# Score pass of the first batch in three attention stages: each score product made three times into the same bank

## The reference, cut to what matters

```python
q = split_heads(queries @ Wq + bq)          # 16 heads of 8
k = split_heads(keys @ Wk + bk)
scores = jnp.einsum('bhqd,bhkd->bhqk', q, k) / jnp.sqrt(jnp.float32(HD))
scores = jnp.where(mask, jnp.float32(-1000000000000000.0), scores)
attn = jax.nn.softmax(scores, axis=-1)
ctx = jnp.einsum('bhqk,bhkd->bhqd', attn, v)
```

## Time and profile before

| what | value |
|---|---|
| median of three runs | 1589.42 us (1583.72 to 1591.42) |
| the profiled execution, its time | 1584.89 us |
| its span, first to last instruction | 1581.8 us |
| mean granted PE clock over the span | 0.94 of 2.4 GHz |
| PE busy | 88% of the span |
| DVE, ACT, POOL busy | 65%, 54%, 34% |
| share of the chain that ended last: PE, DVE, POOL | 67%, 12%, 10% |

### The profile page before, as it was taken

The page is one execution under the profiler, slowest core; times in us unless marked ns, Lnnn a source line. Parts: engine busy times, 40 slices in busy tenths (PEclk is TensorE's granted clock), DMA queues, the critical chain, the costliest instruction groups (busy, mean ns, idle before and its releaser), DMA issues.

```text
span 1581.8 us, 21944 instructions
## 1 busy us (share of the span) xinstructions
PE 1386.6 (88%) x7201; PEld 1099.5 (70%) x7201; DVE 1028.4 (65%) x2075; ACT 850.9 (54%) x1608; POOL 545.0 (34%) x880
## 2 busy tenths in 40 slices
PE   3899798798999999889999997699989989875992
PEld 3565576554888888756678885588878878765992
DVE  4545678755666666845567775577777877655773
ACT  1244566355555555334577775456656666443661
POOL 6723511512233325332201103332333343332674
PEclk7699899799999999989999998889999999986996
DMA  6130232122622323311122100310000000133963
GB/s 153 33 92 2 61 114 94 41 80 63 193 101 99 113 88 120 103 38 61 45 50 107 54 1 1 118 42 1 1 12 5 1 16 1 36 139 117 382 249 87
DMA packets 67790, 123.13 MB, mean 78 GB/s; under 512 B 10200, under 2 KB 43792, under 8 KB 66399
## 3 DMA queue, kind: packets, MB, share of 16 engines
q1 hardware_dynamic: 40495, 104.57, 20.0%
q10 hardware_dynamic: 24688, 12.70, 3.0%
q0 software_dynamic: 2496, 4.47, 0.8%
HBM read 82.61 MB, written 29.16 MB: 71 GB/s over the span
## 4 chain that ended last, share of the span: by engine, by line
PE 67%; DVE 12%; POOL 10%; issue 7%; ACT 2%; DMA 2%; ACTq 0%; POOLq 0%; DVEq 0%; SPq 0%
PE psum L2003 11%; PE psum L2005 11%; PE psum L2004 11%; PE psum L2248 5%; PE psum L2388 4%; PE psum L2390 4%; PE psum L2389 4%; PE psum L2483 3%; PE psum L2201 2%; PE psum L2202 2%; POOL y_dram L994 2%; POOL slots_dram L963 2%; DMA shared<-in_mask_dram 1%; PE psum L2028 1%; PE psum L2232 1%
## 5 line engine op out<-in xcount | busy, mean ns | idle before, releaser
L1816 DVE TENSOR_TENSOR hhl<-psum,hhl 128x512 fp32r<-128x512 f32 x336 | 230.2, 686 | 83.6 <-ACT hhl L1282 81.5
L1282 ACT ACTIVATE hhl<-psum 128x512 fp32r<-128x512 f32 x336 | 199.3, 593 | 3.4 <-DVE psum L1812 3.2
L2003 PE MATMUL psum<-xh,wl 128*128 128x512 f32 x464 | 189.2, 408 | 3.2 <-DVE hhl L1816 2.5
L2004 PE MATMUL psum<-xl,wh 128*128 128x512 f32 x464 | 184.7, 398 | 0.0
L2005 PE MATMUL psum<-xh,wh 128*128 128x512 f32 x464 | 184.4, 397 | 0.0
L1062 POOL TENSOR_SCALAR shared<-shared,xstat 128x589 f32<-128x589 f32 x128 | 97.7, 765 | 232.4 <-DVE xstat L1906 231.9
L1272 ACT ACTIVATE psum<-psum 128x512 f32<-128x512 f32 x208 | 120.9, 582 | 71.3 <-PE psum L2005 70.0
L1354 ACT ACTIVATE hhl<-psum 128x512 fp32r<-128x512 f32 (+1 forms) x160 | 95.4, 596 | 116.9 <-PE psum L2483 116.6
L2388 PE MATMUL psum<-hhl,wl 128*128 128x512 f32 x336 | 135.0, 402 | 12.8 <-DVE xn L1836 9.4
L1812 DVE TENSOR_TENSOR psum<-act_out,psum 128x512 f32<-128x512 f32 x128 | 89.0, 696 | 84.0 <-PE psum L2005 78.5
L1911 DVE TENSOR_TENSOR hhl<-psum,hhl 128x512 fp32r<-128x512 f32 (+1 forms) x160 | 110.3, 689 | 49.6 <-ACT hhl L1354 49.0
(11 more groups left out here) (404 smaller groups left out, 3605.4 us busy)
## 6 DMA issues: line engine op xcount, KB each, us to landing
w3late<-w_dram SPq DMA_DIRECT2D x24, 768.0 KB, 7.2
abkb<-w_dram SPq DMA_DIRECT2D x18, 768.0 KB, 7.4
w_dram<-shared SPq DMA_DIRECT2D x16, 768.0 KB, 5.9
shared<-comb_dram SPq DMA_DIRECT2D x10, 1024.0 KB, 4.7
slots_dram<-late ACTq DMA_DIRECT2D x1, 9792.0 KB, 36.6
shared<-comb_dram SPq DMA_DIRECT2D x24, 256.0 KB, 5.0
late<-in_f_dram SPq DMA_DIRECT2D x8, 768.0 KB, 5.4
shared<-in_f_dram SPq DMA_DIRECT2D x8, 768.0 KB, 8.0
```

Source lines behind the costliest of these rows:

```text
L1282: a.activation(hh[k % 4], h_bank(f, k), ACT.Copy).then_inc(f.hh_done, 1)
L1816: v.tensor_tensor(hl[k % 4], h_bank(f, k), hh[k % 4].bitcast(f32), ALU.subtract).then_inc(f.h_ready, 1)
L2003: mm(dst, ll, rh, start=start, stop=False)
L2004: mm(dst, lh, rl, start=False, stop=False)
```

## The change

For batch 0 of each of the three stages, each score product is preceded by two more of the same operands into the same bank. Each of the three starts afresh (`start=True`), so the first two are overwritten, and the mask product is added to the third as before. Nothing is removed or moved, and no wait is added.

```diff
                         dst = bank(o + j, GW)
+                        if b == 0:
+                            for again in range(2):
+                                mm(dst, qst(l, b)[0:KS, 2 * half + j, tq], kst[0:KS, b, half, at:at + GW],
+                                   start=True, stop=True)
                         mm(dst, qst(l, b)[0:KS, 2 * half + j, tq], kst[0:KS, b, half, at:at + GW], start=True, stop=False)
                         ins = mm(dst, maskT[:, mask_slot(l, b), tq], spreadb[:, 0:GW], start=False, stop=True)
```

## The result

The changed kernel took 1591.44 us (median of 20 runs, 1586.00 to 1595.18) against 1585.78 for the kernel before (20 runs beside it, 1580.78 to 1592.95). The ratio is 1.0034 with a 95% interval of 1.0019 to 1.0049, so it is slower by 5.4 us, between 3.0 and 7.8. In the first three runs the kernel before had its median at 1589.42; the forecast was 1597 us, which was 7.5 us on top of that. The absolute number is therefore 5.6 us too high, of which 3.6 us is that first median; the shift is 2.1 us too large.

What follows compares the result with a forecast made beforehand. PE, busy 88% of the span and 67% of the chain, was taken to bound the kernel. Stages 3.0 + 2.6 + 2.6 = 8.2 us, less 0.7 for the clock, gave 7.5 on 1589.4: 1597 us, range 1588 to 1606.

Steps and rivals of the forecast that it cites:

- The price of a product and the count: Batch 0 steps: 96 added products, each 0.142 us at full clock and 0.26 at low; 13.7 to 25.0 us in all.
- rival of low price: All three stages: nothing is hidden and every step costs 1.04 us, up to 25 us, 1614 in total; chance 0.07.
- What hides: Stage 1 step 0 hides in PE's 3.10 us wait; stage 2 step 0 in 0.81, steps 1 and 2 in 0.92.
- Stage 0: Batch 0 steps of stage 0: nearly all added time on the path; 3.0 us, between 0.4 and 6.0 by the clock.
- Stages 1 and 2: Batch 0 steps there: 2.6 us each, from 2.3 to 3.5 in stage 1 and 2.3 to 3.7 in stage 2.
- Step 7 adds 0.57 ... 2.3 to 3.5: End of stage 1: step 7 adds 0.57 us and gets 0.8 back if the clock holds longer, or adds 1.04.
- The clock given back: Start of the second pass: how long the clock stays low there; 0.7 us taken off the sum.
- the clock holds: Hand-over to the second pass: busier PE keeps the clock from falling in any stage; -2.8 us, 1586.6; chance 0.17.
- a delay was absorbed later: Behind the stages: PE waits later for POOL or a transfer, where the shift ends; 0 to 3 us, 1591; chance 0.12.

Runs made afterwards that it cites:

- again: The changed kernel once more, unaltered, against the kernel before: ratio 1.0034 (1.0014 to 1.0054, 12 runs), +5.4 us.
- again2: The changed kernel a third time, unaltered, against the kernel before: ratio 1.0067 (1.0043 to 1.0091, 6 runs), +10.6 us.
- five: Each score product of batch 0 five times instead of three, 192 products added, against the kernel before: ratio 1.0134, +21 us.
- batch1: The 96 extra products in the steps of batch 1 instead of batch 0, against the kernel before: ratio 1.0065, +10.3 us.
- early: Extra products only in steps 0 to 2 of stages 1 and 2 (24 products), against the kernel before: ratio 1.0002 (0.9983 to 1.0020).
- s0: Extra products in stage 0 alone (32 of the 96), against the kernel before: ratio 1.0031, +4.9 us.
- s12: Extra products in stages 1 and 2 alone (64), against the kernel before: ratio 1.0017, +2.7 us.
- free: No extra products; POOL's first weight splits of stages 1 and 2 wait until DVE has split batch 0's maxima; against the kernel before: ratio 0.9967.
- free_triple: The extra products of the change, with POOL's splits of stages 1 and 2 waiting for batch 0's maxima, against the kernel before: ratio 1.0028, median 1591.09 us.
- fill: No tripling; POOL's splits wait, and unread score products fill PE's waits at batch 0's hand-over; against the kernel before: ratio 0.9954, 7.3 us faster.
- narrow: The changed kernel's 96 extra products only 8 columns wide, against the kernel before: ratio 1.0084, +13.3 us.

## Why the prediction came out as it did

**The price of a product and the count** were right: 0.14 us at full and 0.26 us at low clock, 96 of them.

**Readings.** One figure of the prediction is misread: of the first 25 us of stage 0 some 22 are at low clock by its own rows (43.0 to 47.9 and 51.3 to 68.3), not 17. It stood only as an argument for the rival of low price.

**What hides** was right for the waits. Step 0 of stage 1 left 2.53 of its 3.10 us wait, and step 3 of stage 2 stood 4.96 us after step 0 (4.97 before). It was incomplete for the hand-over.

**Stage 0**, taken as 3.0 between 0.4 and 6.0: the traces give 1 to 8 us over before, on the mean 4.3. Its argument that the clock would hold longer came true in two of five traces. The upper bound was too low, because I let the rise stand at 5 us after step 0, and it came at 10 us in one. Where the clock did hold, 0.4 us was expected and 1 to 2.5 us measured; 2.3 us of the chain were then the two DVE instructions under POOL's L1021.

**Stages 1 and 2**, taken as 2.6 each: this is the step that failed. "Step 7 adds 0.57 ... 2.3 to 3.5" follows PE to the end of the last step and lets everything behind move with it. The step held no term for DVE's two instructions being rounded to the end of a POOL instruction. Measured were 3.7 or 0.2 us in stage 1, and 3.4 in stage 2. In stage 2 the last maxima came 2.4 us later, as the sum had it (2.3), and the two DVE instructions took 3.2 us instead of 2.2 under POOL's splits, which makes 3.4. The rows of before had the sign: an L1703 of 1.4 us whose median is 0.22. I listed it among DVE's pieces of the hand-over and didn't ask what held it.

**The clock given back** was put at 0.7 us. It is the term that was mis-sized, and the one that left the forecast too high. The granted clock of a whole execution, averaged over all runs of a kernel, was 0.936 to 0.937 before (23, 35 and 23 runs) and 0.940, 0.939 and 0.938 after (20, 12 and 6). Among the 20 runs of the changed kernel an execution at 0.943 took 1586.0 and 1587.1 us and those at 0.938 and 0.939 mostly 1592 to 1595; a straight line through the 20 gives 1.2 us for 0.001. The kernel before gives the same 1.2 in each of its three sets of 23 to 35 runs (clocks from 0.932 to 0.942, correlation -0.92 to -0.93). The size is plausible: 0.001 of the mean clock over 1590 us is 3.2 us of low clock, in which PE does half of what it does at full, so at most 1.6 us. By this line 0.003 is worth some 4 us, and at equal clock the change would cost 9 us or more. An estimate for each run, the difference of the means to the kernel before, brought to equal clock by 1.2 us for 0.001:

```
run           means, us    clock        at equal clock, us
again          +6.6        +0.0029      +10.0
again2         +9.8        +0.0015      +11.5
five          +21.7        +0.0005      +22.3
batch1        +10.0        +0.0026      +13.1
early          +0.0        +0.0005       +0.6
s0, s12        +5.8, +2.3  -0.0005, +0.0018   +5.2, +4.4
free           -4.1        +0.0016       -2.2
free_triple    +5.7        +0.0023       +8.3
fill           -7.9        +0.0095       +3.3
narrow        +12.2        -0.0053       +6.0
```

Read so, a dose costs 10 to 12 us whether POOL's splits meet DVE or not (again; free_triple over free), the second dose about as much as the first, batch 1 nearly the price of 13.7, and the gain of fill over free comes from the clock: its products aren't free, they are more than paid back. Half of what the narrow products cost is their low clock. But the line is a correlation within runs, and for fill it is used outside the clocks it was drawn from: no experiment set the clock alone. So the rival "the clock holds" was half right: it doesn't hold through the hand-over in most traces, yet a part of the price seems to come back this way.

**The sum.** Stages 4.3 + 2.3 + 3.4 = 10.0; start and stretches between +0.5; behind stage 2 -1.9 (900.6 against 902.5, with some 2.4 us less low clock). That is the 8.7 us by which the traced spans differ on the mean. The runs say 5.4, 5.4 and 10.6. The traced executions of the changed kernel were on the slow side (mean 1595.3 us against medians of 1591.4, 1593.2 and 1597.3), and had a mean clock of 0.938 against 0.940 over the 20 runs, worth some 2 us by the line, which explains part of the rest. Where a typical execution saves the remaining 1 to 3 us was not settled. The traces show no wait in which a delay was absorbed later: from the second pass of stage 0 to step 0 of stage 1 it was 223.1 us on the mean before and 223.2 after, and from the second pass of stage 1 to step 0 of stage 2 it was 356.4 and 356.2.

The forecast ended near the right shift by luck, through errors of both signs: stages too cheap by 2 us, which is the step that failed, and clock given back too little by about 3, which is an estimate.

## What to carry to other kernels

Before a delay is passed on along a chain, look at each instruction behind it whose duration is far from its own median: something may hold it, and then the delay is rounded up or down to the end of that. Where the clock is in play, compare the mean granted clock over many runs before naming the price of work added to PE; one trace doesn't show it. In this kernel, waits at a hand-over filled with wide products came with a higher clock and no longer time, and a splitting job on POOL belongs behind short DVE instructions on the path: the two together made this kernel 7.3 us faster.

## What the runs showed of the hardware

Products of 8 columns cost 0.12 us each at full clock, not much less than the 0.14 us for 308 columns with weights of the same kind, and the kernel with them had the lower clock although PE's records were busier (22.75 of 29.00 us against 17.73 of 24.90). A DVE cast of 0.2 us lasted up to 2.73 us beside POOL's splits and 0.18 us when these waited. And stage lengths often fall into few values that repeat to 0.05 us between executions and chips (21.30, 22.71; 24.87, 21.35): with the clock and the meeting, small delays come in steps.
